# Late value products, a split attention mask, per-graph GpSimd steps and residual sums kept in PSUM, in a six-layer graph-attention kernel

## The reference

```
# layer 0: 8 heads of 32        (once)
q, k, v = x @ Wq + bq, x @ Wk + bk, x @ Wv + bv
h = softmax(where(adj == 0, -inf, q_h @ k_h.T * scale)) @ v_h   # for each head
x = layernorm(h @ Wo + bo + x) * gamma + beta
# layer 1: one head of 256      (once)
x = layernorm(x + softmax(mask(x Wq (x Wk).T)) @ (x Wv) @ Wo + bo) * gamma + beta
# layers 2 to 5: one head, q and k of width 128, values are x itself
x = layernorm(x + softmax(mask(q @ kk.T / sqrt(128))) @ x @ Wc.T) * ln_g + ln_b
```

## Time and profile before

| | |
|---|---|
| time, median of 3 (lowest, highest) | 2556.24 us (2555.07, 2557.42) |
| profiled execution, its own time | 2563.42 us |
| span of the profiled execution, first to last instruction | 2561.6 us |
| busy: PE, DVE, ACT, POOL | 93%, 70%, 62%, 73% of the span |
| mean granted TensorE clock | 0.984 of full speed |

### The profile page before, as it was taken

One profiled execution on the slowest core, in us unless ns is written; L12 is line 12 of the kernel. 1 busy time (PEld: TensorE's weight loads), 2 busy tenths in 40 slices (PEclk: granted clock), 3 DMA queues, 4 the chain that ended last, 5 costly groups with the idle time before them and its releaser, 6 DMA issues.

```text
span 2561.6 us, 57112 instructions
## 1 busy us (share of the span) xinstructions
PE 2378.7 (93%) x20944; PEld 2201.7 (86%) x20944; DVE 1782.8 (70%) x4874; ACT 1593.2 (62%) x5512; POOL 1862.4 (73%) x2439
## 2 busy tenths in 40 slices
PE   5899999999999999999999999999999999999995
PEld 4788898898898898898888898898898898898884
DVE  2567767777767767767777777777767777767773
ACT  4566666666666666666666666666666666666652
POOL 3577777777777777777777777778777778777773
PEclk8999999999999999999999999999999999999997
DMA  3000000000000000000000000000000000000000
GB/s 139 22 22 22 28 26 22 28 26 22 28 26 22 28 26 22 28 26 22 28 26 22 28 26 22 28 26 22 28 26 20 30 26 22 28 26 16 14 9 13
DMA packets 38150, 68.62 MB, mean 27 GB/s; under 512 B 4336, under 2 KB 12656, under 8 KB 37232
## 3 DMA queue, kind: packets, MB, share of 16 engines
q1 hardware_dynamic: 37872, 64.97, 7.5%
HBM read 48.18 MB, written 16.78 MB: 25 GB/s over the span
## 4 chain that ended last, share of the span: by engine, by line
PE 78%; POOL 11%; DVE 8%; issue 1%; ACT 1%; DMA 0%; POOLq 0%; SPq 0%; DVEq 0%
PE qk_bank L373 15%; PE value_bank L382 15%; PE context_bank L523 9%; PE unit_bank L373 7%; PE qk_bank L478 5%; PE unit_bank L435 4%; PE unit_bank L456 4%; PE unit_bank L382 3%; PE score_bank L507 3%; POOL x_out L919 3%; POOL x_out L921 3%; PE unit_bank L425 3%; PE unit_bank L447 2%; DVE y L796 2%; PE score_bank L514 2%; PE score_bank L504 2%
## 5 line engine op out<-in xcount | busy, mean ns | idle before, releaser
L815 DVE TENSOR_SCALAR y<-y,mv,rstd 128x256 f32<-128x256 f32 x768 | 513.9, 710 | 298.8 <-POOL rstd L900 298.8
L373 PE MATMUL qk_bank<-xT_hi,w_lo 128*128 128x256 f32 x1280 | 406.1, 317 | 121.6 <-DVE xT_lo L761 121.6
L619 ACT CAST xT_hi<-qk_bank 128x512 fp32r<-128x512 f32 x320 | 189.9, 594 | 455.4 <-PE qk_bank L478 455.4
L919 POOL TENSOR_TENSOR x<-y,rows 128x512 f32<-128x512 f32 x320 | 407.8, 1274 | 88.5 <-DVE y L815 85.3
L921 POOL TENSOR_TENSOR x<-x,rows 128x512 f32<-128x512 f32 x320 | 411.7, 1287 | 25.1
L599 ACT ACTIVATE probs<-unit_bank,negmax 128x128 f32<-128x128 f32 x1024 | 365.4, 379 | 60.4 <-DVE negmax L733 60.4
L373 PEld LDWEIGHTS qk_bank<-xT_hi,w_lo 128*128 128x128 f32 x1280 | 242.7, 190 | 178.2 <-DVE xT_lo L761 172.7
L382 PE MATMUL value_bank<-w_lo,xT_hi 128*128 128x256 f32 x1280 | 393.3, 307 | 0.0
L905 POOL TENSOR_TENSOR probs<-probs,rtotal 128x256 f32<-128x256 f32 x512 | 318.2, 643 | 74.5 <-DVE rtotal L746 74.5
L382 PE MATMUL value_bank<-w_hi,xT_lo 128*128 128x256 f32 x1280 | 366.3, 286 | 0.0
L382 PE MATMUL value_bank<-w_hi,xT_hi 128*128 128x256 f32 x1280 | 365.8, 286 | 0.0
(11 more groups left out here) (89 smaller groups left out, 6469.0 us busy)
## 6 DMA issues: line engine op xcount, KB each, us to landing
x0T<-xT_in SPq DMA_DIRECT2D x64, 256.0 KB, 2.6
x<-x_in SPq DMA_DIRECT2D x64, 256.0 KB, 2.7
out<-x_out SPq DMA_DIRECT2D x64, 256.0 KB, 2.1
adj<-adj_in SPq DMA_DIRECT2D x64, 128.0 KB, 2.2
rows<-rows_in SPq DMA_DIRECT2D x1, 1920.0 KB, 11.6
probs0T<-w_in SPq DMA_DIRECT2D x1, 1024.0 KB, 4.9
probs<-w_in SPq DMA_DIRECT2D x1, 1024.0 KB, 8.0
x<-w_in SPq DMA_DIRECT2D x1, 1024.0 KB, 14.0
```

The costliest lines, as they stand in the source:

```text
L373: mm = pe.matmul(psum[:, n * G * N:(n + 1) * G * N], split(w, name, kd, at, at + P), flat(xT_half[:, kd]), start=kd == 0 and w is w_lo, st ...
L815: m = dve.tensor_scalar(y[:, r, g], y[:, r, g], mv[:, r, g, 0:1], rstd[:, r, g:g + 1], ALU.subtract, ALU.mult)
L919: pool.tensor_tensor(new, y[:, r], row_of_each(f"gamma{layer}"), ALU.mult).then_inc(zg_ready, 1)
```

## The change

Four edits in one. (1) The value product of the layer 2 item (r=4) leaves slot r=4 and goes to the next slot, behind `score(i-1)`; ACT moves its result behind the softmax of the same slot. (2) `score0` is cut in two: the mask matmuls and all its waits stay (`open_scores0`), the 16 score matmuls go behind `project_qk(i)`. (3) Residual sums of layers 1 to 5 are written back to `context_bank`, statistics and normalisation read them there, and the next context product waits for `z_ready` where it waited for `y_ready`. Layer 0's stay in `y`. (4) POOL's gamma and beta steps take one graph at a time: four instructions of 128x256 in place of two of 128x512, and `z_ready` and `zg_ready` count graphs.

```diff
+def late_values(i):
+
+    return i % PERIOD == STEP
...
-            def score0(group):
+            def open_scores0(group):
 
                 pe.wait_ge(v0_ready, group + 1)
                 pe.wait_ge(q0_ready, group + 1)
...
                 for j in range(QUAD):
                     pe.matmul(unit_bank[j][:, :], eye16[:, :],
                               mask[:, group % HELD].unsqueeze(2).to_broadcast([P, G, QUADS, N]),
                               start=True, stop=False)
+
+            def score0(group):
                 for g in range(G):
                     for quad in range(QUADS):
                         for j in range(QUAD):
...
                 pe.wait_ge(v_ready, after(i))
                 if NTH[i] > 0:
-                    pe.wait_ge(y_ready, G * (NORM_AT["item", ITEMS[NTH[i] - 1]] + 1))
+                    pe.wait_ge(z_ready, G * (NORM_AT["item", ITEMS[NTH[i] - 1]] + 1))
...
                 if item(i - 1):
                     score(i - 1)
+                if item(i - 1) and late_values(i - 1):
+                    project_v(i - 1)
                 if (group := due(i, 6)) is not None:
-                    score0(group)
+                    open_scores0(group)
...
                 if item(i):
                     project_qk(i)
+                if (group := due(i, 6)) is not None:
+                    score0(group)
...
-                if item(i):
+                if item(i) and not late_values(i):
                     project_v(i)
...
-                if item(i - 1) and item(i - 1)[0] != 1:
+                if item(i - 1) and item(i - 1)[0] != 1 and not late_values(i - 1):
                     move_v(i - 1)
...
                 if item(i - 1):
                     softmax(i - 1)
+                if item(i - 1) and late_values(i - 1):
+                    move_v(i - 1)
...
+            def summed(norm, g):
+
+                if norm[0] == "group":
+                    return y[:, NORM_AT[norm] % YS, g]
+                return context_bank[:, g * D:(g + 1) * D]
+
+            def wait_for_y(norm):
+                at = NORM_AT[norm]
+                if at >= YS:
+                    dve.wait_ge(zg_ready, G * (AFFINE_AT[NORMS[at - YS]] + 1))
...
-                if at >= YS:
-                    dve.wait_ge(zg_ready, AFFINE_AT[NORMS[at - YS]] + 1)
-                for g in range(G):
-                    dve.scalar_tensor_tensor(y[:, r, g], psum[:, g * D:(g + 1) * D], factor[:, g:g + 1],
+                if layer == 0:
+                    wait_for_y(norm)
+                for g in range(G):
+                    dve.scalar_tensor_tensor(summed(norm, g), psum[:, g * D:(g + 1) * D], factor[:, g:g + 1],
                                              kept[:, g], ALU.mult, ALU.add).then_inc(y_ready, 1)
...
-                    last = note(dve.bn_stats(bn[:, r, g], y[:, r, g]))
+                    last = note(dve.bn_stats(bn[:, r, g], summed(norm, g)))
...
-                for g in range(G):
-                    m = dve.tensor_scalar(y[:, r, g], y[:, r, g], mv[:, r, g, 0:1], rstd[:, r, g:g + 1],
-                                          ALU.subtract, ALU.mult)
-                m.then_inc(z_ready, 1)
+                if norm[0] == "item":
+                    wait_for_y(norm)
+                for g in range(G):
+                    dve.tensor_scalar(y[:, r, g], summed(norm, g), mv[:, r, g, 0:1], rstd[:, r, g:g + 1],
+                                      ALU.subtract, ALU.mult).then_inc(z_ready, 1)
...
-                pool.wait_ge(z_ready, NORM_AT[norm] + 1)
-                pool.tensor_tensor(new, y[:, r], row_of_each(f"gamma{layer}"), ALU.mult).then_inc(zg_ready, 1)
-                pool.wait_ge(zg_ready, AFFINE_AT[norm] + 1)
-                pool.tensor_tensor(new, new, row_of_each(f"beta{layer}"), ALU.add).then_inc(x_ready, 1)
+                for g in range(G):
+                    pool.wait_ge(z_ready, G * NORM_AT[norm] + g + 1)
+                    pool.tensor_tensor(new[:, g], y[:, r, g], row(f"gamma{layer}"), ALU.mult).then_inc(zg_ready, 1)
+                for g in range(G):
+                    pool.wait_ge(zg_ready, G * AFFINE_AT[norm] + g + 1)
+                    m = pool.tensor_tensor(new[:, g], new[:, g], row(f"beta{layer}"), ALU.add)
+                m.then_inc(x_ready, 1)
```

More of the change, by code:

```diff
@@ L262, in split, with row @@
             return which[:, at + kd * width + lo:at + kd * width + (width if hi is None else hi)]
+        def row(name):
+            return rows[:, ROWS.index(name), :]
         def row_of_each(name):
```

## The result

The changed kernel takes 2796.59 us (median of 4, 2792.16 to 2798.01), the kernel before 2556.83 us beside it. The ratio is 1.0934, 95% interval 1.0915 to 1.0953. The forecast had the sign and the chain of waits in r=4, but it said 2714 us and at most 2753; 43 us above that end something had been left out. The profiled execution has a span of 2795.8 us, 234 us more than before.

The account below looks back on a forecast made before the run. PE was taken to bound the kernel, with one 1.76 us gap a period in r=0. 62 periods x 2.61 us = 162, less 3.5, gave +158 us: 2714 us on the median, 6.2% slower, range 2666 to 2753.

Parts of the forecast that it names:

- The chain of r=4: Moved scores, row maxima, exponentials, q and k copy, `transpose_x` in series; PE idle 0.97 us before the product, then 2.97 us.
- the walk: One period followed through all engines' lists: 2.03 us longer by PE and ACT, 2.61 with POOL.
- three hand-overs of 0.05: Delays between engines from `exp0` of unit 1 to PE's product in r=0, about 0.05 us each.
- the clock fully granted: PE's steady period before the change, read from the windows: 38.25 us, PE busy 36.49 us, at full clock.
- POOL's term: POOL's work from `x_out` to unit 1, 8.57 us, delays PE in r=1: 2.61 us a period, 0.58 beyond PE and ACT.
- I take 2.45: Time in us assumed for four POOL gamma or beta instructions of 128x256, between estimates of 2.38 and 2.56.
- The bound above it, 2.56: Upper estimate in us for POOL's four short instructions, from 1.28 us for 128x512; used in rival 2.
- rival 1: PE and ACT's chain without POOL's: period grows by 2.03 us, 2679 us; chance 0.22.
- Rival 2: Sums written to PSUM cost +0.2 us each and POOL's four take 2.56: 3.23 us a period, 2753 us; chance 0.14.
- Late values and sums in PSUM: Value product covers 1.49 of the 1.76 us gap in r=0; r=4's normalising pair falls from 2.70 to 0.88 us.
- the rule that the prediction weighed: DVE reads fp32 from PSUM at single rate; r=3's pair would grow 0.40 us, not 0.15, adding 15 us in total.
- Rival 3: Faster: ACT's q and k copy in r=4 finds its turn as before, only r=0's gap goes; 2447 us, chance 0.07.

Follow-up runs that it names:

- all_out_later_fill: `all_out_later` with 24 matmuls of no use ahead of `transpose_x` in r=4; 2697.54 us, ratio 1.0544 to the kernel before.
- all_out_later: Changed kernel with POOL's `x_out` steps moved, gamma to the hole of r=3, beta to r=2 of the next period; 2794.34 us, ratio 1.0922 to the kernel before.
- fill: Changed kernel with 24 matmuls of no use ahead of `transpose_x` in r=4, POOL's steps unmoved; 2756.01 us, ratio 1.0764 to the kernel before.
- apart_only: Kernel before with edit 2 alone: layer 0's score matmuls moved behind `project_qk`; 2737.21 us, ratio 1.0678.
- copy_first: Changed kernel with the q and k copy ahead of unit 0's exponentials on ACT in r=4; 2754.41 us, ratio 1.0764 to the kernel before.

## Why the prediction was wrong

- **The chain of r=4** was right link by link: gaps 0.93 and 2.81 us for 0.97 and 2.97; row maxima, exponentials and `transpose_x` within 0.26 us of the walk. With clock and POOL out of the way (`all_out_later_fill`) the steady period is 40.48 us against 38.28 of before with the clock up: 2.20 us more, where the walk had 2.03. (The walk says three hand-overs of 0.05 and adds 0.10, which is 0.05 of it.)
- **The clock was left out: this is the step that failed.** The prediction says "the clock fully granted" of the steady period, priced r=0 with durations at full clock (0.44, 0.55, 1.49, 0.78), and named the gap of 2.97 us right ahead of it. No term, rival or bound allowed for a fall. It costs 1.56 us a period on average: `all_out_later` and `all_out_later_fill`, which differ in the filling alone, are 97 us apart. The period of the earlier trace rows shows no fall, but the trace of before has 9 of them, behind its gap of 1.76 us and at 1.56 us each; the period just ahead of the one it read has one.
- **POOL's term was mis-sized too.** The step is "I take 2.45". It leaned on the pair of 1.19 us for the probabilities, whose second input is one number a row of 128, and the gamma and beta rows are full inputs: 2.75. The bound above it, 2.56, was too low as well, and both lie below the 2.58 that the two long instructions take in its own rows (1039.67 to 1042.25). The whole chain from `x_out` to the end of unit 1 was 8.98 us and not 8.57. `fill` minus `all_out_later_fill` is 58 us, 0.94 us a period, where the walk had 0.58.
- **How the two lie over each other.** They bound the same stretch, so they don't add. With the clock up and POOL as it is (`fill`) the time is 2756 us, 42 above the forecast: that is the chain and POOL mis-sized. The clock on top makes the other 41. The other way round, with POOL out and the clock falling (`all_out_later`), the time is 2794, within 2 us of the changed kernel: the clock by itself covers POOL's term whole. Even so the 13 periods with the clock up are 41.5 us long, not the 40.9 of the forecast. These parts are differences between the same few runs and close by themselves; what supports the 1.56 from outside is the kernel before.
- **Its signs.** "If PE's wait for POOL in r=0 and r=1 is missing, rival 1": it is missing in 46 of 59 periods, and rival 1's time of 2679 us did not come. The wait was hidden because PE itself came late. Rival 2's signs are absent: the residual sums take 0.48 us each, as before.
- **Late values and sums in PSUM** did what the text says (gap of r=0 closed, pair of r=4 0.99 us), but late values are not free beside edit 2: with the value product in r=4 (`apart_only`) the gap ahead of `transpose_x` is 1.38 us and the clock falls in 5 periods, without it the gap is 2.81 us and the clock falls in 46. `apart_only` is 59 us below the changed kernel; how much of that is the late values and how much POOL's short steps was not tried. The pair that reads PSUM is 0.99 us where 0.88 was taken and 0.73 was before; of the rule that the prediction weighed from the Trainium skill, VectorE: DVE Perf Modes, "Why PSUM operands drop a tier", the direction holds, but the pair grew by 0.26 us and not by the 0.40 us estimated from that page.
- **The rivals**: rival 1 (no POOL) leaves out the clock as well; with both out of the way, `all_out_later_fill` is 18 us above its 2679. Rival 3, faster, named the order on ACT; in `copy_first` that order is changed and the chain is as long.

## What to carry to other kernels

Before moving work from ahead of a step to behind it on one engine, follow the next instruction of every other engine's list that waits for it: the 1.1 us of matmuls were cheap, but their readers stood ahead of the q and k copy on ACT. A gap that such a move opens is priced twice on TensorE, once as idle time and once by the clock behind it; where a gap of some 3 us can't be avoided, matmuls of no use in it may pay (3.5% with POOL's chain out of the way, 1.5% without). One period at full clock doesn't show that all are: look at several. And when a bound is removed, walk the second one first: each of edits 1, 3 and 4 by itself shortened the gap it aimed at and won next to nothing, and edit 3 won its 51 us when POOL's `x_out` steps were out of the way. Edits 1 and 4 were not tried alone with these steps moved.

## What the runs showed of the hardware that was not expected

- TensorE fell to 0.58 of full clock for 4 us behind a gap of 2.8 us, though it was busy 89% of the span. Not every gap does it. Of the steady periods, the clock fell in or just behind a gap of 1.76 us in 9 of 57 (before), with 1.90 us in 21 of 58 (`copy_first`), with 2.07 us in 5 of 58 (`apart_only`), with 2.81 us in 46 of 59 (changed kernel) and 48 of 59 (`all_out_later`). The gap's length alone doesn't order them, as 1.90 and 2.07 us show; what else decides was not tried.
- A GpSimd multiplication of 128x256 takes 0.73 us with two full inputs and 0.62 with one broadcast along the row.
- What VectorE pays for GpSimd's neighbourhood goes by the length of GpSimd's instruction: the pair of SBUF normalisations is 2.70 us beside instructions of 1.28 us, 1.54 beside shorter ones, 0.73 alone, and from PSUM 0.99 whatever GpSimd does.
